# Pooling's softmax weights spread to channels in fp32, and the gram blocks handed from VectorE to ScalarE and GpSimd

## The chip, the cores and the metric

The kernel runs on one core of one Trainium2 chip. The metric is the device time of one execution in microseconds (us), the median of several runs. The trace is that of one profiled execution; all its times are counted from the start of its span.

## The reference

The input is 128 batches of 64 channels by 750 time points. A first layer (`tok`) pads time to 752, cuts it into 94 windows of 8, takes a score for each time point (64 channels times one weight vector, plus a bias), a softmax over the 8 points of a window, and sums the 8 points with those weights:

```python
scores = jnp.einsum('bwkf,of->bwko', xp, w) + b
weights = jax.nn.softmax(scores, axis=2)
pooled = jnp.sum(xp * weights, axis=2)          # 128 x 94 x 64
```

The pooled tokens go through a layer norm, q, k and v projections, an attention of 8 heads that mixes plain, squared and Grassmann scores (which need an orthogonalisation of q and k, and so their gram matrices), a second layer norm and a routed feed-forward network. All of it is fp32. The change touches the pooling and the gram matrices only.

## The kernel before

The program is a row of blocks with a barrier of all engines between them: `constants`, `pool_project`, `orthogonalise`, `attend`. The change is in `pool_project`, with its selector prepared in `constants`.

Two batches of 64 channels make a pair of 128 partitions; there are 64 pairs, in 4 groups of 16. A group's input (`x_g`, two buffers) comes by four DMAs of four pairs each on SyncE's queue. TensorE forms the scores of a group (`score_pair`, line 50), ScalarE copies them out with the bias, VectorE and ScalarE make the softmax of the group at once in `soft`, 64 rows of 376 time points: row 32·half + batch holds one half of the time of one of the group's 32 batches.

The loop of `pool_project` has 32 steps (and 4 more to empty it), two pairs to a step, an even and an odd one. In step i:

- TensorE's `spread` (line 386) carries the weights of one pair from the rows of `soft` to the 64 channels of each of its batches, by a product with a selector of zeros and ones, `pair_sel`: 128 channels, two halves of 376 columns, each in a bank of its own of `ps_spread`. It is called for the even pair, then for the odd one. In the first three groups, while n is below 10, it is followed by one or two score pairs of the next group.
- VectorE multiplies the even pair by the spread weights in PSUM (`product`, line 589) and sums the windows of 8 (`pooled`, line 593). ScalarE copies the odd pair's weights out (`w_odd`, line 493), GpSimd multiplies (line 557), VectorE sums these a step later.
- Each two steps a chunk c of 4 pairs passes the layer norm and the projection, in stages: `centre` (line 398, TensorE) at odd steps; squares and a copy (`j_xc`) on ScalarE; `variance` (404), the square root `j_std` on ScalarE (507), its inverse on VectorE (606), `rows` (415) twice and VectorE's scaled copy into `tok` (618) twice at the even step after; `grams` (427) at the next odd step, 8 gram blocks of 8 by 8 per pair column in `ps_c`.
- The gram blocks stand inside larger products. VectorE's `gram_own` (625) multiplies 256 columns of `ps_c` by `mask4`, and `gram_sum` (630) adds the four groups into `gram`. The next chunk's `centre` overwrites `ps_c`, so it waits for `gram_own`.
- SyncE stores each chunk's `tok` to DRAM by three DMAs, and at the end of the block waits for the last.

Each engine runs its instructions in the order written; the order within a step is TensorE: spread (even), variance and rows 0 or grams, spread (odd), rows 1 or centre; VectorE: product, inverse and rows, pooled odd, gram_own, pads, pooled even, gram_sum, rows, and at i % 8 in (4, 5) the two parts of the next group's softmax.

The weights are fp32 and the products of `spread` are bf16. So `parted` splits them exactly into three bf16 parts: ScalarE writes "hi" (line 456), GpSimd the remainder (459), ScalarE "mid" (462) and its copy to rows 64 to 127 (464), GpSimd "lo" (467). `spread` then makes, for each half, two accumulating products of 128 rows with a 128-row selector. For the first group this chain stands ahead of the first `spread`; for the others it runs at steps i % 8 of 5 and 6.

Of the kernel before, what the change touches and what calls it, by code (L numbers as in the profile page):

```python
# [22 lines left out]
WIN = 8  # L23
# [31 lines left out]
def constants(nc, p, x_g, x_in, ps_score, k):  # L55

    sem = nc.semaphore
    with ExitStack() as ctx:
# [11 lines left out]
        row_sel = ctx.enter_context(nc.sbuf_tensor("row_sel", [128, 2, 32], F32))  # L70
# [36 lines left out]
        def _(pool):  # L107
# [180 lines left out]
def pool_project(nc, x, x_g, x_in, ps_score, tokens, gram, v_dram, qk_dram, top_dram, qk_rows, rows_in, k):  # L288
# [4 lines left out]
    with ExitStack() as ctx:  # L293
        names = ("lo_zero scores_done scores_out maxima shifted exps sums_done inv_done weights_done hi_done rest_done "
                 "mid_done mid_moved lo_done spread_done even_done even_pooled odd_out odd_done odd_pooled "
                 "ready cent_done squared kept var_done std_done rstd_done tok_done gram_done gram_owned")
# [3 lines left out]
        biased = [drained[h] if EVICT[h] == "dve" else ctx.enter_context(sem(f"biased{h}")) for h in range(2)]  # L300
# [7 lines left out]
        soft = sb("soft", [64, N // 2, WIN])  # L308
        rest = sb("rest", [64, HALF])
        mid = sb("mid", [64, HALF], BF16)  # L310
        stat = sb("stat", [64, 3, N // 2])
        parts = sb("parts", [128, 2, 2, HALF], BF16)
# [6 lines left out]
        own = sb("own", [128, 2 * CP, D, 4])  # L319
# [4 lines left out]
        flat = soft[:].rearrange("p w k -> p (w k)")  # L324
# [13 lines left out]
        def _(sp):  # L338
# [6 lines left out]
            def store(c):  # L345
                a, batches = c % 2, slice(2 * CP * c, 2 * CP * (c + 1))
                for h in range(2):
                    sp.wait_ge(biased[h], c + 1)
# [22 lines left out]
        def _(pe):  # L371
# [47 lines left out]
            def grams(c):  # L419
                for h in range(2):  # L420
                    pe.wait_ge(biased[h], c + 1)
# [9 lines left out]
            pe.wait_ge(s["lo_zero"], 1)  # L431
# [19 lines left out]
        def parted(eng, g, part):  # L451

            a = g % 2
            if part == "hi":
                eng.wait_ge(s["weights_done"], g + 1)
                eng.activation(parts[0:64, a, 0, :], flat, ACT.Copy).then_inc(s["hi_done"], 1)
            if part == "rest":
                eng.wait_ge(s["hi_done"], g + 1)
                eng.tensor_tensor(rest[:], flat, parts[0:64, a, 0, :], ALU.subtract).then_inc(s["rest_done"], 1)
            if part == "mid":  # L460
                eng.wait_ge(s["rest_done"], g + 1)
                eng.activation(mid[:], rest[:], ACT.Copy).then_inc(s["mid_done"], 1)
                eng.wait_ge(s["mid_done"], g + 1)
                eng.activation(parts[64:128, a, 0, :], mid[:], ACT.Copy).then_inc(s["mid_moved"], 1)
            if part == "lo":
                eng.wait_ge(s["mid_done"], g + 1)
                eng.tensor_tensor(parts[0:64, a, 1, :], rest[:], mid[:], ALU.subtract).then_inc(s["lo_done"], 1)  # L467

        @block.scalar
        def _(act):  # L470
            def softmax(g, part):
                if part == 0:
                    if g:
                        act.wait_ge(s["scores_done"], g)
                    for quarter in range(4):
                        rows = slice(32 * quarter, 32 * quarter + 32)
                        half, at = divmod(quarter, 2)
                        out = act.activation(flat[32 * half:32 * half + 32, at * (TP // 4):(at + 1) * (TP // 4)], ps_score[rows, 0:TP // 4],
                                             ACT.Identity, bias=k["tok_bias"][rows])
                    out.then_inc(s["scores_out"], 1)  # L480
                if part == 1:
                    act.wait_ge(s["shifted"], g + 1)
                    act.activation(soft[:], soft[:], ACT.Exp).then_inc(s["exps"], 1)
# [25 lines left out]
            def scaled(c, h):  # L509
                a = c % 2  # L510
                if h == 0:
                    act.wait_ge(s["rstd_done"], c + 1)
                if c >= 2:
                    act.wait_ge(stored[a], 48 * (c // 2))
                    act.wait_ge(s["gram_done"], c - 1)
                act.wait_ge(s["tok_done"], 2 * c + h + 1)
                for e in range(2):
                    for b in range(2):
                        r = 2 * h + e
                        out = act.activation(tok[:, a, r, b, :], ps_tok[:, b, 192 * e:192 * e + 192], ACT.Copy,  # L520
                                             scale=rstd[:, a, 2 * r + b:2 * r + b + 1])
                out.then_inc(drained[h], 1)

            for part in range(4):
                softmax(0, part)
            for i in range(STEPS + 4):
                c = chunk_at(i, 4)
                if c is not None:
                    deviation(c)
                    if EVICT[0] == "act":  # L530
                        scaled(c, 0)
                if i < STEPS:
                    odd_weights(i)
                if c is not None and EVICT[1] == "act":
                    scaled(c, 1)
# [3 lines left out]
                if i < STEPS - HP:  # L539
                    for part in {4: (0, 1), 5: (2,), 6: (3,)}.get(i % HP, ()):  # L540
# [3 lines left out]
        def _(pool):  # L544
            def bias(c, h):
                rows = tok[:, c % 2, 2 * h:2 * h + 2].rearrange("p r b f -> p (r b) f")
                pool.wait_ge(drained[h], c + 1)
                pool.tensor_tensor(rows, rows, k["bias_row"][:, 0:1, :].broadcast_to([NP, 4, 192]), ALU.add).then_inc(biased[h], 1)

            pool.memset(parts[64:128, :, 1, :], 0.0).then_inc(s["lo_zero"], 1)  # L550
            parted(pool, 0, "rest")
            parted(pool, 0, "lo")
            for i in range(STEPS + 4):
# [4 lines left out]
                c = chunk_at(i, 4)  # L558
                for h in range(2):
                    if c is not None and EVICT[h] == "act":  # L560
                        bias(c, h)
# [1005 lines left out]
```

## Time and profile before

| | |
|---|---|
| runs, us | 887.52, 888.25, 890.45 (median 888.25) |
| profiled execution, us | 884.84 |
| its span, us | 883.0 |
| mean granted clock of TensorE | 0.937 |
| busy, us (share of span) | TensorE 765.8 (87%), VectorE 721.0 (82%), GpSimd 492.6 (56%), ScalarE 447.0 (51%) |
| `pool_project` in the trace | about 26 to 230.5 us |

The profiled execution took 884.84 us, 1.84 us of it outside the span from the first to the last instruction, and lies 3.41 us under the median of the runs. Busy shares are means over blocks with different limits, so the block that the change touches is read by itself. A granted clock of 1.00 is TensorE's upper level (2.4 GHz), 0.50 its lower (1.2 GHz).

### The profile page before, as it was taken

The numbers are of one execution on the slowest core, as the hardware profiler recorded it, in microseconds if no ns is written. First come the engines' busy times: TensorE is split into PE (matmuls) and PEld (weight loads), VectorE is DVE, ScalarE is ACT, GpSimd is POOL, SyncE is SP. The second block draws the span as 40 slices with busy tenths as digits, with TensorE's granted clock in tenths as the row PEclk, the third lists the DMA queues.
The fourth block names the chain that finished last, engine by engine and source line by source line (L and its number), as shares of the span: only waits on it lengthen the run. The fifth ranks groups of instructions, "written<-read, shape, count | busy, mean of one in ns | idle before, by whom it ended". The sixth has DMA issues, their size and how long they took to land.

```text
span 883.0 us, 39788 instructions
## 1 busy us (share of the span) xinstructions
PE 765.8 (87%) x16837; PEld 565.1 (64%) x16837; DVE 721.0 (82%) x1408; ACT 447.0 (51%) x927; POOL 492.6 (56%) x532
## 2 busy tenths in 40 slices
PE   4488887666694599999999999999999999899994
PEld 2245444434674478877777778877777887466663
DVE  4388888885579589999999999999999999667772
ACT  2253424321344165565655565665565556477773
POOL 3233333331000578888888888888888887222220
PEclk9789899896697599999999999999999999899998
DMA  8756662662570122222222222222222221001111
GB/s 295 284 168 198 197 197 58 130 128 58 155 143 2 48 76 64 65 64 64 64 66 65 79 65 64 64 64 64 66 73 71 64 64 45 1 22 29 28 29 33
DMA packets 89197, 77.63 MB, mean 88 GB/s; under 512 B 37145, under 2 KB 79708, under 8 KB 89052
## 3 DMA queue, kind: packets, MB, share of 16 engines
q1 hardware_dynamic: 88524, 73.83, 28.9%
q8 instruction: 131, 2.15, 1.0%
q10 hardware_dynamic: 528, 1.54, 0.5%
q14 instruction: 14, 0.11, 0.0%
HBM read 59.23 MB, written 13.04 MB: 82 GB/s over the span
## 4 chain that ended last, share of the span: by engine, by line
PE 51%; DVE 10%; issue 3%; ACT 1%; POOL 0%; POOLq 0%; ACTq 0%; DVEq 0%
PE ps_dot L1116 10%; PE ps_m L1140 8%; PE ps_a L1166 7%; PE ps_a L1158 7%; PE ps_a L1252 4%; DVE row_max_o L1376 3%; DVE row_max_e L1378 3%; PE ps_a L1129 3%; DVE row_max L1364 2%; PE ps_m L1102 2%; PE ps_a L1237 2%; DVE sums L1396 2%; PE ps_dot L1209 1%; PE ps_a L1260 1%; PE ps_dot L1227 1%
## 5 line engine op out<-in xcount | busy, mean ns | idle before, releaser
L1295 ACT ACTIVATE sq<-ps_dot 128x376 f32<-128x376 f32 x384 | 165.0, 482 | 158.4 <-PE ps_dot L1116 150.4
L1116 PE MATMUL ps_dot<-q_st,k_blk 64*64 64x94 f32 x6144 | 170.5, 249 | 1.1 <-ACT sq L1295 0.8
L1116 PEld LDWEIGHTS ps_dot<-q_st,k_blk 64*64 64x64 f32 x6144 | 134.6, 134 | 52.8 <-issue 28.8
L557 POOL TENSOR_TENSOR x_g<-x_g,w_odd 128x752 f32<-128x752 f32 x32 | 57.0, 1780 | 104.4 <-ACT w_odd L493 104.4
L1038 POOL TENSOR_TENSOR v_blk<-v_rep,vmask 128x384 f32<-128x384 f32 x128 | 106.6, 854 | 7.6 <-PE ps_m L1146 5.5
L1053 POOL TENSOR_TENSOR half<-prob 128x564 f32<-128x564 f32 x64 | 75.6, 1181 | 60.7 <-ACT prob L1290 60.7
L1060 POOL TENSOR_TENSOR k_blk<-k_cm,hmask 128x768 f32<-128x768 f32 x64 | 96.7, 1511 | 1.0 <-PE ps_a L1158 1.0
L1062 POOL TENSOR_TENSOR k_mix<-k_cm,cols 128x768 f32<-128x768 f32 x64 | 96.8, 1512 | 0.0
L1364 DVE TENSOR_REDUCE row_max<-ps_a 128x94 f32<-128x564 f32 x128 | 89.4, 740 | 4.5 <-PE ps_a L1166 4.4
L1166 PE MATMUL ps_a<-sq,mix_w 64*32 64x282 f32 x2048 | 81.8, 404 | 0.5 <-ACT sq L1295 0.5
L1140 PE MATMUL ps_m<-prob,v_blk 128*64 128x94 f32 x1536 | 76.6, 248 | 1.1 <-ACT prob L1290 1.1
L1287 ACT ACTIVATE prob<-prob,head_const 128x564 f32<-128x564 f32 x64 | 49.1, 767 | 51.7 <-DVE prob L1386 51.7
L1158 PE MATMUL ps_a<-q_st,k_mix 64*64 64x94 f32 x3072 | 74.3, 241 | 0.8 <-issue 0.4
L1140 PEld LDWEIGHTS ps_m<-prob,v_blk 128*64 128x64 f32 x1536 | 64.8, 136 | 8.7 <-ACT prob L1290 1.7
L1089 POOL COPY w_sel<-ffn_w 128x258 f32 x64 | 25.7, 402 | 79.5 <-DVE qk_rows L1452 54.2
L1158 PEld LDWEIGHTS ps_a<-q_st,k_mix 64*64 64x64 f32 x3072 | 67.2, 133 | 1.2 <-issue 1.1
L1371 DVE TENSOR_TENSOR k_blk<-ps_m,hmask 128x768 f32<-128x768 f32 x64 | 61.3, 957 | 7.5 <-PE ps_dot L1116 4.9
L386 PE MATMUL ps_spread<-parts,pair_sel 128*128 128x376 bf16 x256 | 58.4, 356 | 10.0 <-POOL parts L467 10.0
L493 ACT ACTIVATE w_odd<-ps_spread 128x752 f32<-128x752 f32 x32 | 25.5, 797 | 80.8 <-PE ps_spread L386 80.6
L1046 POOL TENSOR_TENSOR m_blk<-m_t,mask 128x128 f32<-128x128 f32 x64 | 25.8, 404 | 63.9 <-POOLq L706 63.9
L1396 DVE TENSOR_REDUCE sums<-half 128x94 f32<-128x282 f32 x128 | 59.8, 469 | 1.7 <-POOL half L1053 1.7
L593 DVE TENSOR_REDUCE tokens<-x_g 128x94 f32<-128x752 f32 x64 | 59.0, 925 | 0.6 <-POOL x_g L557 0.4
(219 smaller groups left out, 1450.7 us busy)
## 6 DMA issues: line engine op xcount, KB each, us to landing
v_rep<-v_rows SPq DMA_DIRECT2D x128, 192.0 KB, 3.1
x_g<-in_x_dram SPq DMA_DIRECT2D x15, 1500.0 KB, 6.5
qk_rows_kept<-tok SPq DMA_DIRECT2D x16, 384.0 KB
qk_rows<-qk_rows_kept SPq DMA_DIRECT2D x4, 1536.0 KB, 11.2
v_rows<-tok SPq DMA_DIRECT2D x16, 192.0 KB
q_st<-q_cm SPq DMA_DIRECT2D x64, 47.0 KB, 1.8
out_dram<-rows SPq DMA_DIRECT2D x16, 188.0 KB
x_g<-in_x_dram ACTq DMA_DIRECT2D x1, 1500.0 KB, 7.1
```

The lines of the kernel that those rows point to most:

```text
L1038: vb = pool.tensor_tensor(v_blk[:, a, b].rearrange("p t (o d) -> p (t o) d", o=H), v_rep[:, a, b].rearrange("p (t o d) -> p (t o) d", o=H, ...
L1053: pool.tensor_tensor(half[:], prob[:, a, :, 0:3, :], prob[:, a, :, 3:6, :], ALU.add).then_inc(s["half_done"], 1)
L1060: pool.tensor_tensor(k_blk[:, a, :, 0], k_cm[:, span(i, 1), :].rearrange("p i (u m) -> p (i u) m", m=4).unsqueeze(2).broadcast_to([128, NT ...
L1062: pool.tensor_tensor(k_mix[:, a].rearrange("p t x o -> p (t x) o"), k_cm[:, span(i, 1), :].rearrange("p i m -> p (i m)").unsqueeze(2).broa ...
L1116: mm = pe.matmul(ps_dot[64 * v:64 * v + 64, (2 * g + b) % 3, N * c:N * c + N], k_blk[rows, a, SLOTS * (3 * v + g) + c].rearrange("p k h m ...
L1140: pe.matmul(ps_m[64 * b:64 * b + 64, AV_AT:AV_AT + N], v_blk[:, a, b, t, :], prob[:, a, b, t, :], start=(t == 0), stop=(t == NT - 1), skip ...
L1158: mm = pe.matmul(ps_a[half_of, BANK[b][t // 3], N * (t % 3):N * (t % 3) + N], k_mix[64 * b:64 * b + 64, a, t, 8 * w:8 * w + 8].rearrange(" ...
L1166: mm = pe.matmul(ps_a[32 * c:32 * c + 32, BANK[b][v], 0:3 * N], k["mix_w"][64 * v:64 * v + 64, :], sq[64 * v:64 * v + 64, b, c].rearrange( ...
L1295: act.activation(sq[:, b, :, g, :], ps_dot[:, (2 * g + b) % 3, 0:SLOTS * N].rearrange("p (c n) -> p c n", c=SLOTS), ACT.Square).then_inc(s ...
L1364: dve.tensor_reduce(top[:, b, :], bass.AP(ps_a[:].tensor, 1024 * b, [[4 * 512, 128], [1, N], [512, 2], [N, 3]]), AX.XY, ALU.max).then_inc( ...
L1371: dve.tensor_tensor(k_blk[:, a, :, 1], ps_m[:, KT_AT:KT_AT + NP].rearrange("p (u m) -> p u m", m=4).unsqueeze(2).broadcast_to([128, NT * S ...
L1396: dve.tensor_reduce(sums[:, b], half[:, b].rearrange("p t n -> p n t"), AX.X, ALU.add).then_inc(s["sums_done"], 1)
```

## The change

`pair_sel` becomes fp32, 64 rows of 16 by 128. `spread` makes one fp32 product per half, whose operands are the 32 rows of that half: half 0 on rows 0 to 31, half 1 on rows 32 to 63, each into its own bank as before. The splitting (`parted`, its five instructions a group, and a memset) goes away; `soft` gets a second buffer, since `spread` now reads it directly. ScalarE copies the 256 gram columns out of PSUM (`grams_out`, first in its odd step), GpSimd masks them in place and adds them in two halvings (`gram_sum`, after its product with the odd pair); `centre` waits for ScalarE's copy in place of VectorE's masked one. The choice of engine for the scaled copy (`EVICT`), which was VectorE for both halves, is written out as such.

```diff
@@ constants
-            for quarter in range(4):
-                diagonal(row_sel[32 * quarter:32 * quarter + 32, quarter % 2, :], 0, [[-1, 32]], 1)
+            for half in range(2):
+                diagonal(row_sel[32 * half:32 * half + 32, :], 0, [[-1, 32]], 1)
...
-            for half in range(2):
-                act.activation(k["pair_sel"][:, half].rearrange("p n (b c) -> p (n b) c", b=2),
-                               row_sel[:, half, :].unsqueeze(2).broadcast_to([128, 32, C]), ACT.Copy)
+            act.activation(k["pair_sel"][:].rearrange("p n (b c) -> p (n b) c", b=2),
+                           row_sel[:].unsqueeze(2).broadcast_to([64, 32, C]), ACT.Copy)
@@ pool_project, TensorE
-                    pe.wait_ge(s["mid_moved"], g + 1)
-                    pe.wait_ge(s["lo_done"], g + 1)
+                    pe.wait_ge(s["weights_done"], g + 1)
...
                 for half in range(2):
-                    for part in range(2):
-                        mm = pe.matmul(ps_spread[:, 2 * (n % 2) + half, 0:HALF], k["pair_sel"][:, half, n, :], parts[:, g % 2, part, :],
-                                       start=(part == 0), stop=(part == 1))
+                    mine = slice(32 * half, 32 * half + 32)
+                    mm = pe.matmul(ps_spread[:, 2 * (n % 2) + half, 0:HALF], k["pair_sel"][mine, n, :], flat[mine, g % 2, :], start=True, stop=True)
...
-                    pe.wait_ge(s["gram_owned"], c)
+                    pe.wait_ge(s["gram_out"], c)
@@ ScalarE
-                if part == 2:
-                    parted(act, g, "hi")
-                if part == 3:
-                    parted(act, g, "mid")
...
+            def grams_out(c):
+                act.wait_ge(s["gram_done"], c + 1)
+                if c:
+                    act.wait_ge(s["gram_summed"], c)
+                act.activation(own[:].rearrange("p b g e -> p (b g e)"), ps_c[:, 0:256], ACT.Copy).then_inc(s["gram_out"], 1)
...
             for i in range(STEPS + 4):
+                c = chunk_at(i, 5)
+                if c is not None:
+                    grams_out(c)
@@ GpSimd
-            parted(pool, 0, "rest")
-            parted(pool, 0, "lo")
+            def gram_sum(c):
+                pool.wait_ge(s["gram_out"], c + 1)
+                pool.tensor_tensor(own[:], own[:], k["mask4"][:].unsqueeze(1).unsqueeze(3).broadcast_to([128, 2 * CP, 4, D]), ALU.mult).then_inc(s["gram_owned"], 1)
+                pool.wait_ge(s["gram_owned"], c + 1)
+                pool.tensor_tensor(own[:, :, 0:2], own[:, :, 0:2], own[:, :, 2:4], ALU.add).then_inc(s["gram_halved"], 1)
+                pool.wait_ge(s["gram_halved"], c + 1)
+                pool.tensor_tensor(gram[:, span(c, 2 * CP), :], own[:, :, 0, :], own[:, :, 1, :], ALU.add).then_inc(s["gram_summed"], 1)
...
-                if i < STEPS - HP and i % HP == 5:
-                    parted(pool, i // HP + 1, "rest")
-                if i < STEPS - HP and i % HP == 6:
-                    parted(pool, i // HP + 1, "lo")
+                c = chunk_at(i, 5)
+                if c is not None:
+                    gram_sum(c)
@@ VectorE
-                c = chunk_at(i, 5)
-                if c is not None:
-                    gram_own(c)
...
-                c = chunk_at(i, 5)
-                if c is not None:
-                    gram_sum(c)
```

## Rows read from the trace of the kernel before

**Rows 1.** Busy time of each engine in three stretches of pooling (instructions, granted clock).
```profile
35.90:41.90 6.00, 6.00 (x63) 2.24 (x60) 3.28 (x4) 1.22 (x2) 1.78 (x1) 0.77 0.27 106
104.00:113.00 9.00, 7.82 (x32) 4.70 (x34) 6.86 (x15) 4.21 (x8) 2.87 (x3) 0.50 0.40 124
163.00:205.00 42.00, 29.58 (x425) 17.54 (x424) 35.01 (x72) 10.57 (x20) 14.23 (x8) 0.95 0.66 133
```

**Rows 2.** VectorE's waits, 35 to 205 us: total, times, longest.
```profile
DVE x_g L589 <- PE ps_spread L386: 14.5, 15, 4.7
```

**Rows 3.** Timeline at pooling's start: start us, us, what, idle before.
```profile
31.32 0.54 DVE L584 TENSOR_TENSOR soft<-soft,stat 64x376 f32<-64x376 f32 x1
...
34.01 0.89 POOL L467 TENSOR_TENSOR parts<-rest,mid 64x376 bf16<-64x376 f32 x1 [0.63 <-ACT mid L462]
...
35.14 1.41 PE L386 MATMUL ps_spread<-parts,pair_sel 128*128 128x376 bf16 x4 [10.00 <-POOL parts L467]
```

**Rows 4.** Timeline of one chunk without scores, steps 29 and 30.
```profile
192.00 0.92 DVE L589 TENSOR_TENSOR x_g<-x_g,ps_spread 128x752 f32<-128x752 f32 x1
...
192.18 0.75 PE L427 MATMUL ps_c<-tok 94*32 94x32 f32 x64 [1.58 <-issue]
...
192.87 0.81 PE L386 MATMUL ps_spread<-parts,pair_sel 128*128 128x376 bf16 x4
...
194.25 0.88 PE L398 MATMUL ps_c<-tokens,cent_w 128*128 128x384 f32 x2 [0.57 <-DVE own L625]
...
194.97 0.80 PE L386 MATMUL ps_spread<-parts,pair_sel 128*128 128x376 bf16 x4
...
195.80 0.94 DVE L589 TENSOR_TENSOR x_g<-x_g,ps_spread 128x752 f32<-128x752 f32 x1 [0.54 <-PE ps_spread L386]
...
196.86 0.89 PE L415 MATMUL ps_tok<-w_tok,j_xc 64*96 64x192 f32 x8
...
197.69 0.81 PE L386 MATMUL ps_spread<-parts,pair_sel 128*128 128x376 bf16 x4
197.90 1.39 DVE L618 SCALAR_TENSOR_TENSOR tok<-ps_tok,j_rstd,bias_row 96x192 f32<-96x192 f32 x4 [0.44 <-PE ps_tok L415]
...
202.39 0.92 DVE L589 TENSOR_TENSOR x_g<-x_g,ps_spread 128x752 f32<-128x752 f32 x1
```

**Rows 5.** Groups of instructions, forms apart, 20 to 240 us: busy, mean ns, idle before.
```profile
L501 ACT ACTIVATE j_xc<-ps_c 128x384 f32<-128x384 f32 x16 | 7.8, 486 | 0.0
L625 DVE TENSOR_TENSOR own<-ps_c,mask 128x256 f32<-128x256 f32 x16 | 6.6, 411 | 2.5 <-PE ps_c L427 2.5
```

**Rows 6.** Page, costliest groups: GpSimd's products in the attention.
```profile
L1038 POOL TENSOR_TENSOR v_blk<-v_rep,vmask 128x384 f32<-128x384 f32 x128 | 106.6, 854 | 7.6 <-PE ps_m L1146 5.5
L1046 POOL TENSOR_TENSOR m_blk<-m_t,mask 128x128 f32<-128x128 f32 x64 | 25.8, 404 | 63.9 <-POOLq L706 63.9
```

**Rows 7.** Timelines of two chunks with a softmax, steps 13, 14 and 22.
```profile
103.40 0.80 ACT L493 ACTIVATE w_odd<-ps_spread 128x752 f32<-128x752 f32 x1
...
104.96 1.62 PE L398 MATMUL ps_c<-tokens,cent_w 128*128 128x384 f32 x2 [1.60 <-DVE own L625]
...
107.87 0.94 DVE L589 TENSOR_TENSOR x_g<-x_g,ps_spread 128x752 f32<-128x752 f32 x1 [0.38 <-PE ps_spread L386]
...
110.66 1.39 DVE L618 SCALAR_TENSOR_TENSOR tok<-ps_tok,j_rstd,bias_row 96x192 f32<-96x192 f32 x4 [0.81 <-PE ps_tok L415]
...
155.27 0.20 DVE L606 RECIPROCAL j_rstd<-j_std 96x8 f32<-96x8 f32 x1 [1.31 <-ACT j_std L507]
```

**Rows 8.** TensorE's timeline in step 9, a step with scores.
```profile
81.59 0.84 PE L50 MATMUL ps_score<-x_g,score_w 128*32 128x188 f32 x16
82.37 0.91 PE L398 MATMUL ps_c<-tokens,cent_w 128*128 128x384 f32 x2
```

**Rows 9.** Timeline of the block's end and the barrier behind it.
```profile
227.34 0.42 DVE L630 TENSOR_REDUCE gram<-own 128x64 f32<-128x256 f32 x1
...
230.66 4.16 PE L871 MATMUL ps_turn<-ident,gram 128*128 128x128 f32 x16 [3.83 <-PEq L293]
```

More of the change, by code:

```diff
@@ L299, in pool_project @@
         drained = [ctx.enter_context(sem(f"drained{h}")) for h in range(2)]
-        biased = [drained[h] if EVICT[h] == "dve" else ctx.enter_context(sem(f"biased{h}")) for h in range(2)]
         def sb(name, shape, dt=F32):
@@ L318, in pool_project @@
         tok = sb("tok", [NP, 2, CP, 2, 192])
-        own = sb("own", [128, 2 * CP, D, 4])
+        own = sb("own", [128, 2 * CP, 4, D])
         ps_spread = ctx.enter_context(nc.psum_tensor("ps_spread", [128, 4, 512], F32))
@@ L449, in _ @@
                     centre(c)
[L451 to L467, printed above, removed]
         @block.scalar
@@ L474, in softmax @@
                         act.wait_ge(s["scores_done"], g)
+                    if g >= 2:
+                        act.wait_ge(s["spread_done"], GP * (g - 1))
                     for quarter in range(4):
@@ L477, in softmax @@
                         half, at = divmod(quarter, 2)
-                        out = act.activation(flat[32 * half:32 * half + 32, at * (TP // 4):(at + 1) * (TP // 4)], ps_score[rows, 0:TP // 4],
+                        out = act.activation(flat[32 * half:32 * half + 32, g % 2, at * (TP // 4):(at + 1) * (TP // 4)], ps_score[rows, 0:TP // 4],
                                              ACT.Identity, bias=k["tok_bias"][rows])
@@ L507, in deviation @@
                 act.activation(std[:], ps_c[0:NP, W:W + 2 * CP], ACT.Sqrt, bias=k["ln_eps"][0:NP, 0:1]).then_inc(s["std_done"], 1)
[L509 to L524, printed above, removed]
+            def grams_out(c):
[3 more added lines that the diff above has]
+                act.activation(own[:].rearrange("p b g e -> p (b g e)"), ps_c[:, 0:256], ACT.Copy).then_inc(s["gram_out"], 1)
+            for part in range(2):
                 softmax(0, part)
             for i in range(STEPS + 4):
+                c = chunk_at(i, 5)
+                if c is not None:
+                    grams_out(c)
                 c = chunk_at(i, 4)
@@ L539, in _ @@
                 if i < STEPS - HP:
-                    for part in {4: (0, 1), 5: (2,), 6: (3,)}.get(i % HP, ()):
+                    for part in range(2 if i % HP == 4 else 0):
                         softmax(i // HP + 1, part)
@@ L557, in _ @@
                     pool.tensor_tensor(odd, odd, w_odd[:, i % 2, :], ALU.mult).then_inc(s["odd_done"], 1)
[L558 to L561, printed above, removed]
-                if i < STEPS - HP and i % HP == 5:
-                    parted(pool, i // HP + 1, "rest")
-                if i < STEPS - HP and i % HP == 6:
-                    parted(pool, i // HP + 1, "lo")
+                c = chunk_at(i, 5)
+                if c is not None:
+                    gram_sum(c)
         @block.vector
@@ L574, in softmax @@
                     dve.wait_ge(s["scores_out"], g + 1)
-                    dve.tensor_reduce(stat[:, 0, :], soft[:], AX.X, ALU.max).then_inc(s["maxima"], 1)
+                    dve.tensor_reduce(stat[:, 0, :], soft[:, g % 2], AX.X, ALU.max).then_inc(s["maxima"], 1)
                     dve.wait_ge(s["maxima"], g + 1)
-                    dve.tensor_tensor(soft[:], soft[:], over(stat[:, 0, :]), ALU.subtract).then_inc(s["shifted"], 1)
+                    dve.tensor_tensor(soft[:, g % 2], soft[:, g % 2], over(stat[:, 0, :]), ALU.subtract).then_inc(s["shifted"], 1)
                 if part == 1:
                     dve.wait_ge(s["exps"], g + 1)
-                    dve.tensor_reduce(stat[:, 1, :], soft[:], AX.X, ALU.add).then_inc(s["sums_done"], 1)
+                    dve.tensor_reduce(stat[:, 1, :], soft[:, g % 2], AX.X, ALU.add).then_inc(s["sums_done"], 1)
                     dve.wait_ge(s["sums_done"], g + 1)
@@ L583, in softmax @@
                     dve.wait_ge(s["inv_done"], g + 1)
-                    dve.tensor_tensor(soft[:], soft[:], over(stat[:, 2, :]), ALU.mult).then_inc(s["weights_done"], 1)
+                    dve.tensor_tensor(soft[:, g % 2], soft[:, g % 2], over(stat[:, 2, :]), ALU.mult).then_inc(s["weights_done"], 1)
             def product(i):
@@ L621, in rows_out @@
                 out.then_inc(drained[h], 1)
-            def gram_own(c):
-                dve.wait_ge(s["gram_done"], c + 1)
-                dve.tensor_tensor(own[:], ps_c[:, 0:256].rearrange("p (b g e) -> p b e g", g=4, e=D),
-                                  k["mask4"][:].unsqueeze(1).unsqueeze(1).broadcast_to([128, 2 * CP, D, 4]), ALU.mult).then_inc(s["gram_owned"], 1)
-            def gram_sum(c):
-                dve.wait_ge(s["gram_owned"], c + 1)
-                dve.tensor_reduce(gram[:, span(c, 2 * CP), :], own[:], AX.X, ALU.add)
             softmax(0, 0)
@@ L639, in _ @@
                     inverse(c)
-                    if EVICT[0] == "dve":
-                        rows_out(c, 0)
+                    rows_out(c, 0)
                 if 1 <= i <= STEPS:
                     pooled(i - 1, 1)
-                c = chunk_at(i, 5)
-                if c is not None:
-                    gram_own(c)
                 c = chunk_at(i, 2)
@@ L651, in _ @@
                     pooled(i, 0)
-                c = chunk_at(i, 5)
+                c = chunk_at(i, 4)
                 if c is not None:
-                    gram_sum(c)
-                c = chunk_at(i, 4)
-                if c is not None and EVICT[1] == "dve":
                     rows_out(c, 1)
@@ L659, in _ @@
                     softmax(i // HP + 1, i % HP - 4)
-EVICT = ("dve", "dve")
 def span(c, n):
@@ L1498, in audio_layer @@
             k["score_w"] = first.enter_context(nc.sbuf_tensor("score_w", [128, GP, 32], F32))
-            k["pair_sel"] = first.enter_context(nc.sbuf_tensor("pair_sel", [128, 2, GP, 128], BF16))
+            k["pair_sel"] = first.enter_context(nc.sbuf_tensor("pair_sel", [64, GP, 128], F32))
             ps_score = first.enter_context(nc.psum_tensor("ps_score", [128, 512], F32))
```

30 lines of the change are left out of this document (8 added, 22 removed).

## The prediction

> **What bounds the kernel now.** The chain that ended last reaches back only to 297 us and doesn't enter pooling, so I read pooling by windows first, then by VectorE's waits, then by the order of time in single chunks. From 163 to 205 us VectorE is busy 35.01 of 42.00 us, TensorE 29.58, GpSimd 14.23, ScalarE 10.57 [rows 1]. The reader is to see an engine that is nearly full and yet waits: VectorE lost 14.5 us in 15 waits before `product`, all for `spread` [rows 2]. The rows of one chunk say why [rows 4]. From the product of step 29 (192.00) to that of step 31 (202.39) is a period of 10.39 us. `centre` starts at 194.25, 0.57 us after TensorE was free, when VectorE's `gram_own` is over; the next `spread` stands behind it (194.97), and the next product, at 195.80, has waited 0.54. What follows from `centre` (squares, variance, rows) ends in `rows_out` at 197.90, after 0.44 more. So the period is a ring: VectorE's copies let `grams` start, then spread, gram_own, centre, rows, and VectorE again. Only what shortens this ring shortens the period, not every microsecond taken from VectorE.
>
> Two stretches differ. Before the first chunk TensorE is busy 6.00 of 6.00 us [rows 1]: there it is the bound. And at the start TensorE waits 10.00 us, the last part of it for the splitting: the weights are ready at 31.32 + 0.54 = 31.86, `lo` ends at 34.90, `spread` starts at 35.14 [rows 3].
>
> **The start.** Without the splitting `spread` can follow the weights at about 31.9: 3.2 us earlier. It runs at the lower clock there (1.41 us against 0.81) and will be 0.1 longer, see below. **-3.1 us.** Next due is the second group's input, for the scores behind each spread: from 35.9 us on TensorE is busy without a gap [rows 1], so it was there by then; that it is there 3 us sooner no row shows, and if it weren't the term would be 0.
>
> **The new spread.** Before: four bf16 records of 376 columns, 0.81 us start to end [rows 4]. The trace has no fp32 product of 32 rows. Nearest rows: `centre`, fp32, leaves two records of 384 columns per product, 0.88 us start to end and 0.72 to the next start, or 0.94 ns a column. Two fp32 products of 376 columns one after the other would be 4 x 0.35, about 1.55 us start to end; side by side 0.87. Which of the two, the `rows` product tells: eight fp32 records of 192 columns, in two tiles of 64 rows with a bank each, took 0.89 us [rows 4], where 8 x 0.18 = 1.44 would be their time in turn. They run in pairs. I take 0.87, 0.06 longer than before, and keep 1.55 for the rival.
>
> The shape of the tile changes too. `rows` to `spread` is 0.83 us (196.86 to 197.69) for 4 x 192 columns, which at centre's pace take 0.72: 0.11 us go into a change from 64-row tiles to 128 [rows 4]. Before, `centre`, both spreads around it and `variance` had 128 rows and columns for one another; now each passage is such a change, three more in a chunk, two of them ahead of `variance`.
>
> The Trainium skill (TensorEngine Tiling (Array Packing), Key Properties) says that changing the tiling mode drains the engine, while changing the tile within a mode doesn't. The 0.11 us agrees in kind; if a whole drain were the 0.16 us by which `centre` ends after the next record has started (0.88 - 0.72), two a chunk would cost 0.1 us more than by the row, 1.6 us over 16 chunks, and the sum below would be -5.2.
>
> **Early, TensorE bound.** Some nine spreads by 0.06 and two changes around the first `centre` by 0.11: **+0.8 us**. Bounds 0 and 1.6.
>
> **Chunks without scores.** After the change `centre` waits for ScalarE's copy. `grams` ends at 192.93; the copy of 256 columns costs at most the 0.49 of 384 columns [rows 5], so it is over by 193.45 and hidden by `spread`. `centre` then starts behind it: 192.87 + 0.71 + 0.11 = 193.69 in place of 194.25, 0.56 earlier. Squares, variance and rows follow `centre` with the same delays, so `rows_out` and the period lose 0.56. VectorE has 0.41 + 0.41 less to do; 0.26 of this becomes waiting. Three chunks are of this kind (steps 25, 27, 29): -1.7. In two (7, 15) the even step has scores ahead of `variance`, so the longer spread and its change (0.17) are on the ring: -0.39 each. **-2.5 us.**
>
> **Chunks with scores.** In step 9 `centre` (82.37) follows the score without a wait [rows 8]: gram_own is no part of the ring. What remains are two longer spreads and one more change: +0.23, in steps 9 and 17. In 11 and 19 half as many scores stand there, some of the wait for gram_own is left, and I take +0.1. **+0.7 us**, bounds -0.3 and +1.4.
>
> **Chunks with a softmax (steps 5, 13, 21).** Here `centre` waits 1.60 us for gram_own, as it has the softmax behind it on VectorE [rows 7]. After: ScalarE's copy takes the place that `w_odd` has now, 103.40, right after the exponential; with 0.49 `centre` can start at 103.95 in place of 104.96. `w_odd` moves back 0.4 to 0.5, and GpSimd behind it; the sum that needs them comes a step later. In steps 5 and 13 TensorE has the lower clock (0.50 from 104 to 113 [rows 1], `centre` 1.62 against 0.88), so the added 0.17 doubles: -1.01 + 0.34, and a little more as the copy is shorter than 0.49: -0.75 each. In step 21 the clock is up; there VectorE waits 1.31 for the square root [rows 7], which stands behind `hi` in ScalarE's queue. `hi` goes and `centre` is earlier, so this wait and the two gram instructions (0.74 to 0.82) go: -1.9. **-3.4 us**, bounds -1.5 and -7 (the last if steps 5 and 13 behave as 21).
>
> **Chunks at the lower clock without softmax (23, 31).** `centre` has no wait for gram_own there; spreads and changes at double price: **+0.7 us**.
>
> **At nothing.** GpSimd: three instructions of 256, 128 and 64 columns, by 0.85 (384 columns) and 0.40 (128) [rows 6] between 1.2 and 1.7 us a chunk; in 163 to 205 us it is idle 27.8 of 42, four chunks add 6.6. They stand between two products with the odd pairs; the cover is the wait for `w_odd`, and were it gone, 0.6 us a chunk would delay the odd sums. The splitting at later groups: ready some 3 us before it is needed. The selector in `constants`: ScalarE then waits for the scores anyway. The end: gram_sum on VectorE ends at 227.76, the next block starts at 230.66, held by SyncE's wait for the last store; ScalarE and GpSimd would end near 229 [rows 9]. If the barrier waited for them instead, +1.5.
>
> **The sum.** -3.1 + 0.8 - 2.5 + 0.7 - 3.4 + 0.7 = -6.8 us. Against the profiled execution: 884.84 - 6.8 = 878.0. The median of the runs lies 3.41 us higher, so I expect a median of 888.25 - 6.8 = **881.4 us**. With all added TensorE prices at nothing it would be -10, with twice these prices -3.6: the forecast's own range is 878 to 885.
>
> **Rivals.**
>
> *The halves run in turn* (slower). For it: no row has 32-row tiles, nor only two products in a row; against it: the pairs in `rows`. A spread then costs 0.66 to 0.7 us more. On the ring or on the full TensorE: ten early spreads (6.6), two in each of four chunks with scores (5.3), two at double price in steps 5 and 13 (5.3), five chunks without scores that go from -0.56 to about +0.5 (5.3), steps 21, 23 and 31 (4.5): +27, in all +20, about 908 us. If the second record of the first half overlaps the first of the second (three slots for four), half of it: +6.7, 895 us. It decides from 0.17 us a spread on (6.8 / 27 x 0.66).
>
> *TensorE becomes the bound* (no change). VectorE is relieved, but another part of the ring, such as `variance` behind the longer spread, takes all that the chunks give, -5.9. Left are -3.1 + 0.8 + 0.7 + 0.7 = -0.9: 887 us. For it speaks that in chunks with scores TensorE already has no gap ahead of `centre` [rows 8]; against it the 0.57 and 1.60 us of idle TensorE in the others [rows 4, 7].
>
> *The clock stays up.* Steps 5 and 13 have the lower clock after TensorE sat idle 1.60 us ahead of `centre` and longer before `grams`. With the idle time shorter the clock may not fall: two chunks then give 1.9 and not 0.75, step 23 gains 1 to 2: -4 more, 877 us. Against it: the other gaps of those steps stay, and 32-row tiles may equally leave it low for longer, at about 1.2 us a stretch.
>
> **How the numbers follow.** Forecast 0.60, clock stays up 0.12, TensorE the bound 0.14, halves in turn 0.14 (half of it partly). A change of 0.3%, 2.7 us, is about what a measurement of this kernel can tell from none. Faster by more: the forecast less its upper end, and the third rival, 0.68. Within: the second rival and that upper end, 0.18. Slower: 0.14. The range 875 to 891 holds the forecast, both middle rivals and the bounds, and leaves out most of the halves in turn.
>
> **What would show it.** First `spread` at about 32 us. A spread of 0.85 to 0.95 us at the upper clock with the second half's record starting within some 10 ns of the first's; over 1.2 proves the first rival. No-score periods of 9.8 us; `centre` there right behind `spread`, not behind ScalarE. GpSimd's gram work of 1.2 to 1.7 us inside its wait for `w_odd`. Next block 6 to 8 us earlier than 230.66. The prediction is wrong if periods don't shrink while `centre` starts earlier: then the ring is another one.

## The result and the profile after

| | before | after |
|---|---|---|
| median of the runs, us | 888.87 (4 runs, 887.52 to 890.45) | 928.28 (4 runs, 920.98 to 935.78) |
| profiled execution, us | 884.84 | 921.21 |
| its span, us | 883.0 | 919.3 |
| mean granted clock of TensorE | 0.937 | 0.874 |
| first `spread`, us | 35.14 | 33.15 |
| next block starts, us | 230.66 | 266.80 |

The change made the kernel slower: ratio 1.0362, interval 1.0330 to 1.0393. The prediction (881.4, range 875 to 891) was wrong in sign. Two of the four runs after, those at 935 us with a clock of 0.855 and 0.862, are left out of the ratio. The span grew by 36.3 us and the start of the next block moved by 36.1, so nearly all of it was lost ahead of that start, although the first `spread` came 2.0 us earlier.

The page of after, its row of TensorE's granted clock (40 slices of 23 us), and then windows of after, those of [rows 1] and two more; each line gives the window, its length, the busy time of TensorE, its weight loads, VectorE, ScalarE and GpSimd, the granted clock, and the DMA's share and GB/s:

```profile
PEclk9555958655559859999999999999999999999998
```

```profile
35.90:41.90 6.00, 6.00 (x36) 1.89 (x34) 2.59 (x4) 0.80 (x1) 1.77 (x1) 0.50 0.23 92
104.00:113.00 9.00, 8.21 (x140) 4.71 (x142) 6.75 (x13) 2.47 (x6) 4.83 (x5) 1.00 0.78 242
163.00:205.00 42.00, 40.24 (x352) 21.20 (x352) 28.40 (x55) 14.31 (x26) 16.07 (x18) 0.58 0.39 84
...
35.90:60.00 24.10, 24.10 (x145) 8.78 (x144) 9.79 (x12) 5.34 (x7) 7.07 (x4) 0.50 0.25 87
...
180.00:220.00 40.00, 39.66 (x318) 19.96 (x316) 24.44 (x49) 8.98 (x18) 14.65 (x15) 0.50 0.58 121
```

From 163 to 205 us the clock was 0.95 before, with TensorE busy 29.58 us and VectorE 35.01 [rows 1]; now it is 0.58, TensorE is busy 40.24 and VectorE 28.40. The bound has passed to TensorE. From 36 to 60 us TensorE has no gap at all (24.10 of 24.10 us) and keeps its lower level, 1.2 GHz, throughout. The kernel before, in the same stretch:

```profile
35.90:60.00 24.10, 20.86 (x266) 10.15 (x264) 19.44 (x31) 10.64 (x16) 10.22 (x6) 0.92 0.46 158
```

The clock of after isn't low everywhere: from 104 to 113 us it is 1.00, where before was at 0.50 in another step [rows 1]. Over the whole of pooling the mean is 0.61 after (35.9 to 264 us) and 0.86 before (35.9 to 230).

Was it the new product that took TensorE's time? The groups of TensorE's instructions in pooling, of before and then of after (busy us, mean ns, idle before):

```profile
L386 PE MATMUL ps_spread<-parts,pair_sel 128*128 128x376 bf16 x256 | 58.4, 356 | 10.0 <-POOL parts L467 10.0
L415 PE MATMUL ps_tok<-w_tok,j_xc 64*96 64x192 f32 x256 | 33.5, 387 | 10.2 <-DVE tok L618 9.9
L50 PE MATMUL ps_score<-x_g,score_w 128*32 128x188 f32 x440 | 24.5, 333 | 2.3 <-DMA x_g<-in_x_dram 2.3
L398 PE MATMUL ps_c<-tokens,cent_w 128*128 128x384 f32 x32 | 17.5, 637 | 8.5 <-DVE own L625 8.3
L404 PE MATMUL ps_c<-mean_w,j_sq 128*96 128x2 f32 x128 | 15.1, 239 | 3.2 <-ACT j_xc L501 3.2
```

```profile
L378 PE MATMUL ps_spread<-soft,pair_sel 32*128 32x376 f32 x256 | 89.8, 792 | 6.8 <-DVE soft L539 6.8
L406 PE MATMUL ps_tok<-w_tok,j_xc 64*96 64x192 f32 x256 | 45.5, 498 | 4.1 <-DVE tok L573 3.8
L50 PE MATMUL ps_score<-x_g,score_w 128*32 128x188 f32 x440 | 33.4, 431 | 1.1 <-DMA x_g<-in_x_dram 1.1
L389 PE MATMUL ps_c<-tokens,cent_w 128*128 128x384 f32 x32 | 23.0, 816 | 1.0 <-ACT own L483 1.0
L395 PE MATMUL ps_c<-mean_w,j_sq 128*96 128x2 f32 x128 | 20.6, 283 | 1.9 <-ACT j_xc L471 1.9
```

The four groups that the change doesn't touch took 90.6 us and take 122.5: +31.9, beside +31.4 of `spread`. Instructions that stayed the same and grew by a third point to the clock. (Busy time grew by more than the 36 us lost, as part of it fills time in which TensorE was idle before.)

Now a chunk as in [rows 4], step 25 of after, where the clock is 0.50, and step 9 of after at the upper level, which answers to [rows 8] (timelines):

```profile
196.33 0.94 DVE L544 TENSOR_TENSOR x_g<-x_g,ps_spread 128x752 f32<-128x752 f32 x1
...
197.38 1.62 PE L378 MATMUL ps_spread<-soft,pair_sel 32*128 32x376 f32 x4
197.51 0.38 ACT L483 ACTIVATE own<-ps_c 128x256 f32<-128x256 f32 x1 [3.57 <-PE ps_c L418]
198.94 1.65 PE L389 MATMUL ps_c<-tokens,cent_w 128*128 128x384 f32 x2
...
202.19 0.94 DVE L544 TENSOR_TENSOR x_g<-x_g,ps_spread 128x752 f32<-128x752 f32 x1 [3.23 <-PE ps_spread L378]
...
209.83 0.94 DVE L544 TENSOR_TENSOR x_g<-x_g,ps_spread 128x752 f32<-128x752 f32 x1
```

```profile
98.36 0.91 PE L389 MATMUL ps_c<-tokens,cent_w 128*128 128x384 f32 x2
99.20 0.90 PE L378 MATMUL ps_spread<-soft,pair_sel 32*128 32x376 f32 x4
100.04 0.84 PE L50 MATMUL ps_score<-x_g,score_w 128*32 128x188 f32 x16
```

`grams`' copy is over 197.51 + 0.38 = 197.89, hidden by `spread`, and `centre` follows without a wait, as the prediction had it. At the upper level a spread takes 0.90 us; at the lower 1.62. The period, 196.33 to 209.83, is 13.50 us where it was 10.39 [rows 4], and VectorE waits 3.23 us for `spread` in place of 0.54.

VectorE's waits for `spread` from 35 to 205 us answer to [rows 2] (14.5 us in 15), the groups of the gram work to [rows 6] and the end to [rows 9]:

```profile
DVE x_g L544 <- PE ps_spread L378: 33.5, 13, 4.3
```

```profile
L507 POOL TENSOR_TENSOR own<-own,mask 128x256 f32<-128x256 f32 x15 | 9.7, 648 | 7.8 <-ACT own L483 7.8
L509 POOL TENSOR_TENSOR own<-own 128x128 f32<-128x128 f32 x15 | 7.0, 468 | 1.2
L511 POOL TENSOR_TENSOR gram<-own 128x64 f32<-128x64 f32 x15 | 4.8, 317 | 1.2
...
L483 ACT ACTIVATE own<-ps_c 128x256 f32<-128x256 f32 x15 | 5.7, 383 | 49.2 <-PE ps_c L418 49.1
```

```profile
264.70 0.32 POOL L511 TENSOR_TENSOR gram<-own 128x64 f32<-128x64 f32 x1
...
266.80 1.54 PE L807 MATMUL ps_turn<-ident,gram 128*128 128x128 f32 x5 [3.84 <-PEq L291]
```

### The profile page after: what moved, and what is told of

Read it like the earlier page. It is cut to its first block, busy times and chain, and to the rows that moved or that the text cites. A ratio compares the mean times of both kernels' runs of the same rounds, so it can differ in the third digit from the quotient of the medians.

```text
span 919.3 us, 39808 instructions
## 1 busy us (share of the span) xinstructions
PE 830.0 (90%) x16837; PEld 587.7 (64%) x16837; DVE 713.0 (78%) x1376; ACT 445.5 (48%) x930; POOL 506.4 (55%) x569
## 4 chain that ended last, share of the span: by engine, by line
PE 48%; DVE 10%; issue 3%; ACT 1%; POOL 0%; POOLq 0%; ACTq 0%; DVEq 0%
PE ps_dot L1052 9%; PE ps_m L1076 8%; PE ps_a L1102 7%; PE ps_a L1094 7%; PE ps_a L1188 3%; DVE row_max_o L1312 3%; DVE row_max_e L1314 3%; PE ps_a L1065 3%; DVE row_max L1300 2%; DVE sums L1332 2%; PE ps_m L1038 2%; PE ps_a L1173 1%; PE ps_dot L1145 1%; PE ps_a L1196 1%; PE ps_m L1082 1%
## 5 line engine op out<-in xcount | busy, mean ns | idle before, releaser
L378 PE MATMUL ps_spread<-soft,pair_sel 32*128 32x376 f32 x256 | 89.8, 792 | 6.8 <-DVE soft L539 6.8
L544 DVE TENSOR_TENSOR x_g<-x_g,ps_spread 128x752 f32<-128x752 f32 x32 | 29.9, 934 | 40.6 <-PE ps_spread L378 39.9
L573 DVE SCALAR_TENSOR_TENSOR tok<-ps_tok,j_rstd,bias_row 96x192 f32<-96x192 f32 x128 | 44.4, 406 | 21.7 <-PE ps_tok L406 21.7
```

## The experiments

Each ratio is taken against runs of the kernel before in the same comparison, whose medians were 888.47 us (e1 to e4), 888.00 (e5 to e7) and 887.41 (e8 to e10).

Theory A: the spread that leaves 64 of TensorE's 128 rows out keeps the granted clock at its lower level, and everything on TensorE pays. Theory B: it is the fp32 product itself, its passes, weight loads or changes of tile shape. Theory C: moving the grams changed order and idle time, and so the clock.

### All 128 rows in use (e1_rows128)

After, with the weights on rows 0 to 31 and 64 to 95, and each half a tile of 64 rows; the 32 spare rows of a tile meet zeros in the selector. Columns, data type, weight loads and the records per spread stay; the height of a tile changes from 32 to 64 rows.

```diff
-                    mine = slice(32 * half, 32 * half + 32)
+                    mine = slice(64 * half, 64 * half + 64)
```

> The changed kernel with each half's 32 weight rows placed at the head of a tile of 64 rows (rows 0 to 31 and 64 to 95), the 32 rows behind them zeros in the selector: the two fp32 products of a spread now take all 128 rows of TensorE in place of 64, same columns, same order, same waits. Theory A (the granted clock falls as the new spread leaves half of the rows out): the clock stays at the upper level for most of pooling as before the change, and the time is what was predicted, 876 to 886 us. Theory B (fp32 itself, its weight loads or the more frequent changes of tile shape bring the clock down): nothing changes, 915 to 935 us, with the lower clock in about three quarters of pooling.

892.91 us (9 runs, 888.29 to 895.99), ratio 1.0045, interval 1.0017 to 1.0073, clock 0.913. That is slower than the 876 to 886 that theory A forecast, but by the ratios (1.0362 and 1.0045) 28 of the 32 us are gone. Its stretch from 36 to 60 us and one chunk without scores at the upper level:

```profile
35.90:60.00 24.10, 21.78 (x260) 10.34 (x260) 19.54 (x33) 11.79 (x20) 10.84 (x7) 0.92 0.52 168
```

```profile
197.35 0.90 PE L378 MATMUL ps_spread<-soft,pair_sel 64*128 64x376 f32 x4
198.19 0.91 PE L389 MATMUL ps_c<-tokens,cent_w 128*128 128x384 f32 x2
199.03 0.90 PE L378 MATMUL ps_spread<-soft,pair_sel 64*128 64x376 f32 x4
```

A spread takes the same 0.90 us as with 32-row tiles, so no time was saved in the product itself: the clock is what differs, 0.92 against 0.50. What keeps this kernel from the forecast is the clock too. From 39 to 149.3 us it fell only for up to about 9 us at a time, as before's did; then it fell for 37.6 us, where before's fall of that place, from about 158 to 165 us, lasted some 7 (windows):

```profile
140.00:149.30 9.30, 6.97 (x133) 4.48 (x126) 7.90 (x17) 5.25 (x10) 3.57 (x5) 1.00 0.15 34
149.30:186.90 37.60, 35.36 (x259) 19.51 (x262) 25.40 (x51) 9.77 (x18) 14.88 (x15) 0.50 0.40 86
```

Ahead of the fall TensorE was busy 6.97 of 9.30 us; after it, 35.36 of 37.60. The no-score periods are 13.57 and 13.49 us in the low stretch, 9.89 and 9.87 behind it.

### The old bf16 product on half the rows (e2_before64)

Before, whose products take rows 0 to 63 alone; this leaves out the middle part of the weights.

```diff
-                        mm = pe.matmul(ps_spread[...], k["pair_sel"][:, half, n, :], parts[:, g % 2, part, :],
+                        mm = pe.matmul(ps_spread[...], k["pair_sel"][0:64, half, n, :], parts[0:64, g % 2, part, :],
```

> The kernel before, with its bf16 products of spread on rows 0 to 63 alone (the mid part of the weights is left out; hi and lo stay): as many products and columns, no fp32, no other edit. Theory A: the lower clock takes over in pooling here too and the time rises by 20 us or more, to 905 to 930. Theory B: unchanged within 3 us, 886 to 892.

916.8 us (4 runs, 906.45 to 921.48), ratio 1.0283, interval 1.0225 to 1.0341, clock 0.868:

```profile
35.90:60.00 24.10, 24.10 (x153) 8.30 (x151) 10.85 (x13) 5.34 (x7) 7.07 (x4) 0.50 0.26 92
```

No fp32 spread, no moved grams, no products side by side, the same number of products and columns: the clock falls as in after. This execution was the longest of the four; the others had 0.876 to 0.891, against 0.928 to 0.944 for before. A change of tile shape does come in with the 64-row product, but e1 has 64-row tiles between 128-row products too, with all rows in use, and 0.92 in this window. B and C are not needed for the loss.

### The spread alone and the grams alone (e3_spread_only, e4_grams_only)

After with the grams as before on VectorE; and before with the grams moved as in the diff.

```diff
-                    pe.wait_ge(s["gram_out"], c)
+                    pe.wait_ge(s["gram_owned"], c)
```

> The changed kernel with the grams masked and summed by VectorE as before: the fp32 spread alone. Theory A: the clock of the changed kernel, as the spread is the cause, 920 to 940 us, a few us over the changed kernel or equal to it. Theory C (moving the grams shifted the order of work and so the idle times on which the clock depends): the clock recovers, 880 to 895 us.

> The kernel before with the grams alone moved to ScalarE and GpSimd, bf16 spread and splitting kept. By the prediction's steps the ring of a chunk without scores is 0.6 us shorter (no shape change is added here), chunks with a softmax 1 to 2 us, chunks with scores 0 to 0.2: -6 to -9 us, 880 to 883. Theory C: the clock falls, 915 us or more. If VectorE's relief is all turned into waits: 887 to 890.

The spread alone: 937.54 us (4 runs, 928.57 to 955.32), ratio 1.0494, interval 1.0434 to 1.0554, clock 0.852. The grams alone: 884.08 us (12 runs, 878.34 to 887.58), ratio 0.9940, interval 0.9915 to 0.9964, clock 0.934. The two parts have opposite signs. C falls: the moved grams gain 4.4 us by the medians (5.3 by the ratio), somewhat less than the 6 to 9 expected, and their clock is before's.

### Do the zeros matter? (e5_signed)

As e1_rows128, with +1 and -1 in the selector's spare rows, which cancel.

```diff
+                step(pool.memset(spare, 1.0))
+                step(pool.affine_select(out=spare, in_=spare, compare_op=ALU.is_ge, fill=-1.0, base=-16,
+                                        pattern=[[0, 32]], channel_multiplier=1))
```

> The kernel with two tiles of 64 rows again, but the selector's 32 spare rows of each tile hold +1 (16 rows) and -1 (16 rows) in place of zeros; the spare rows of the weights are all equal, so their share adds up to nothing. Open is why 64-row tiles still have more of the lower clock than the kernel before (0.913 against 0.937) and 893 in place of 881 us. If it is the zeros, the clock comes up to 0.93 or more and the time to 876 to 886 us. If rows in use count whatever stands in them, it stays at 889 to 896, and the rest is to be looked for in the tile shapes or the order of work.

891.22 us (10 runs, 886.47 to 896.05), ratio 1.0044, interval 1.0020 to 1.0069, clock 0.917: as with zeros in the selector. (The spare rows of `soft` hold the softmax of zeros, 1/8 each, in both.) What the selector has in the spare rows makes no difference that these runs can tell; values of the weights in those rows were not varied.

### The splitting hidden at the start only (e6_grams_first)

e4_grams_only, in which the first four pairs are spread in fp32 from two 64-row tiles while the splitting runs beside them. For that `soft` has two buffers and its halves stand at rows 0 and 64, as in e1.

```diff
+                    if g == 0 and n < FIRST:
+                        mine = slice(64 * half, 64 * half + 64)
+                        mm = pe.matmul(ps_spread[...], k["first_sel"][mine, n, :], flat[mine, 0, :], start=True, stop=True)
+                        continue
```

> The kernel before with the grams moved, and in addition the first four pairs alone spread in fp32 from two tiles of 64 rows, so that they need not wait for the splitting, which runs beside them; from the fifth pair on the bf16 products with all rows. The start should come 2 to 3 us earlier than with the grams alone, the clock stay as in the kernel before: 879 to 883 us, ratio about 0.991. If the start is taken back by later waits: 884 as with the grams alone.

881.38 us (7 runs, 874.87 to 882.61), ratio 0.9905, interval 0.9871 to 0.9938, clock 0.939. Against e4 that is 0.0035 of 888 us, about 3.1 us, the size that the prediction gave to the start; the two intervals overlap, so these runs don't prove the gain.

### The halves in turn, on all rows (e7_in_turn)

After with the rows of e1_rows128, but each half an fp32 product over one tile of 128 x 128, with zeros in the selector for the other half's rows. The two halves then run one after the other: this is the first rival of the prediction, built as a kernel.

```diff
-                    mm = pe.matmul(ps_spread[...], k["pair_sel"][mine, n, :], flat[mine, g % 2, :], start=True, stop=True)
+                    mm = pe.matmul(ps_spread[...], k["pair_sel"][:, half, n, :], flat[:, g % 2, :], start=True, stop=True)
```

> The changed kernel with each half's fp32 product over all 128 rows in one tile of 128 by 128 (zeros in the selector outside the half's 32 rows): the two halves must run in turn, and there is no change of tile shape around the centre and variance products. Theory A (rows left out bring the clock down): the clock stays up, a spread takes about 1.55 us, and the time is that of the prediction's rival for halves in turn, 900 to 912 us. If fp32 products bring the clock down by themselves: more than 930 us, a spread of 2.9 us at the lower level.

887.63 us (10 runs, 885.48 to 889.54), ratio 0.9994, interval 0.9973 to 1.0014, clock 0.953; the 900 to 912 that was expected was too much. Two of its windows, and a spread ahead of `centre`:

```profile
35.90:60.00 24.10, 24.10 (x192) 12.34 (x185) 14.12 (x22) 7.68 (x13) 8.36 (x5) 0.95 0.27 92
...
38.20:212.00 173.80, 162.80 (x1904) 95.02 (x1902) 131.03 (x251) 62.30 (x113) 76.27 (x73) 1.00 0.51 141
```

```profile
175.66 1.53 PE L378 MATMUL ps_spread<-soft,pair_sel 128*128 128x376 f32 x4
177.02 0.81 PE L389 MATMUL ps_c<-tokens,cent_w 128*128 128x384 f32 x2
```

The same stretch, TensorE busy the same 24.10 of 24.10 us, fp32 products of 376 columns in both kernels: 0.50 after, 0.95 here. A spread of 1.53 us in place of 0.90 makes a kernel that is some 33 us faster (ratios 0.9994 and 1.0362), since from 38 to 212 us the clock is 1.00 without a break. B falls: e7 has the fp32 products and their passes, e1 the changes of tile shape besides, and neither has the clock of after.

### TensorE's idle time filled (e8_rows128_fill, e9_after_fill, e10_best_fill)

One fp32 product of 128 rows into `ps_c`, whose result nobody reads, stands ahead of `grams` (324 columns, 160 in steps with scores) and, in steps without scores, ahead of the second `rows` (160). In e8 this is added to e1_rows128, in e9 to after, in e10 to e6_grams_first.

```diff
+            def fill(c, columns):
+                pe.wait_ge(s["std_done"], c + 1)
+                pe.matmul(ps_c[:, 0:columns], k["ident"][:], k["w_bd"][:].rearrange("p s f -> p (s f)")[:, 0:columns],
+                          start=True, stop=True)
...
+                        fill(c, 160)
...
+                fill(c, 160 if i < STEPS - HP and i % HP < 5 else 324)
```

> The kernel with two tiles of 64 rows, and idle TensorE filled: one extra fp32 product of 128 rows whose result nobody reads (324 columns ahead of grams, 160 where scores stand in the step, and 160 ahead of the second rows product in steps without scores), put where TensorE waits for VectorE's copies anyway. If that idle time is what still lets the clock fall with all rows in use, the clock stays up through pooling, no-score periods are 9.9 us throughout and the time is 876 to 882 us. If it isn't, 889 to 896 us, with the stretches of the lower clock after steps 5, 13 and 21 as before.

> The changed kernel (tiles of 32 rows) with the same filling products and nothing else. If rows left out by the spread bring the clock down (theory A), the filling, a tenth of TensorE's time, repairs little: 910 to 935 us, clock below 0.89. If idle time had been the cause, the clock recovers and the time is that of the prediction, 876 to 886 us.

> The kernel before with the grams moved and the first four pairs in fp32, with the same filling products. Its six stretches of the lower clock in pooling cost about 1 us each; if they go, 875 to 879 us and a clock of 0.95 or more; if not, 880 to 883 us as without the filling.

| kernel | us (runs) | ratio, interval | clock |
|---|---|---|---|
| e8_rows128_fill | 875.47 (4: 872.67 to 876.32) | 0.9854, 0.9818 to 0.9891 | 0.949 |
| e9_after_fill | 927.34 (4: 911.76 to 928.0) | none given | 0.874 |
| e10_best_fill | 874.58 (6: 867.97 to 877.16) | 0.9849, 0.9811 to 0.9886 | 0.958 |

A window of e1_rows128 and the same one of e8_rows128_fill, then three of e9_after_fill:

```profile
36.90:197.00 160.10, 139.30 (x1751) 76.68 (x1750) 121.00 (x232) 57.71 (x102) 68.44 (x65) 0.82 0.52 145
...
36.90:197.00 160.10, 137.33 (x1940) 76.90 (x1940) 131.38 (x250) 62.74 (x113) 74.97 (x72) 1.00 0.56 154
```

```profile
35.90:60.00 24.10, 24.10 (x148) 8.36 (x140) 10.60 (x13) 5.34 (x7) 7.08 (x4) 0.50 0.28 100
100.00:140.00 40.00, 36.36 (x536) 19.57 (x534) 32.18 (x63) 16.26 (x30) 17.87 (x19) 1.00 0.67 212
180.00:220.00 40.00, 40.00 (x303) 20.42 (x294) 19.58 (x39) 8.54 (x17) 12.89 (x14) 0.50 0.58 120
```

With all rows in use the filling lifts e1_rows128 from 0.82 to 1.00 over the same 160 us and gains 17 us (ratios 1.0045 and 0.9854). With 32-row tiles the runs, 911.76 to 928.0 us against 920.98 to 935.78 for after, show no gain beyond their scatter: the upper level holds from 100 to 140 us, but in the other two windows TensorE has no idle time that could be filled (24.10 of 24.10 us, 40.00 of 40.00) and is at 0.50 all the same. e10_best_fill beats both kernels, by 13 us against before in the same comparison (887.41 - 874.58); e8 does so by 12. Against e6, without the filling, e10's gain is about 5 us by the ratios, and their intervals overlap a little.

## Why the prediction was wrong

**The step that failed** is "The new spread". It weighed how long the product lasts at a given clock (+0.06 us a spread) and let the clock be that of before, stretch by stretch; in its place the mean clock of pooling fell from 0.86 to 0.61, and what the change doesn't touch on TensorE got longer with it (90.6 us to 122.5). That rows left out bear on the clock came up only against the third rival: "32-row tiles may equally leave it low for longer, at about 1.2 us a stretch". The kind was right there and the size wrong: the low stretches did not grow by some us, they became most of pooling. e1 (rows back, same times, 0.92 in place of 0.50 from 36 to 60 us) and e2 (rows taken from the old product, 0.50) show the cause from both sides. Over all the kernels, from 36 to 60 us, the four whose spread takes 64 rows (after, e2, e3, e9) have 0.50, and the eight others 0.87 to 1.00.

**The ring was right at the upper level, in the chunks whose clock before was up too.** Periods between VectorE's `product` in odd steps, each the difference of two starts in the timelines, us; those of e8 and of e1 where its clock was up:

```
chunk of step      5      7      9      11     13     21     25-29
before             12.40  10.45  10.93  11.80  12.44  11.65  10.39
after (mixed)      11.63  15.42  11.22  11.92  12.62  12.61  13.5
e1, upper level      -    10.12  11.22  11.93    -      -    9.87-9.89
e8                 10.04  10.12  11.22  11.93  10.04  10.03  9.86-9.87
predicted change   -0.75  -0.39  +0.23  +0.10  -0.75  -1.9   -0.56
e8 less before     -2.36  -0.33  +0.29  +0.13  -2.40  -1.62  -0.53
```

In chunks 5 and 13 the prediction kept before's lower clock and named -7 for all three softmax chunks if they behaved as step 21, although three times its own -1.9 is -5.7; at the upper level they give -6.4. The filling of e8 stands in these periods too.

**The start** was sized right and partly lost ahead of it. Rows of after's timelines that answer to [rows 3]:

```profile
22.80 2.73 PE L50 MATMUL ps_score<-x_g,score_w 128*32 128x188 f32 x32 [1.14 <-DMA x_g<-in_x_dram]
...
32.51 0.54 DVE L539 TENSOR_TENSOR soft<-soft,stat 64x376 f32<-64x376 f32 x1
...
33.15 1.62 PE L378 MATMUL ps_spread<-soft,pair_sel 32*128 32x376 f32 x4 [6.82 <-DVE soft L539]
```

The first `spread` follows the weights by 0.10 us in place of 3.28 us (32.51 + 0.54 = 33.05, 33.15; before 31.86, 35.14), as forecast, but the weights are 1.19 us later than before's 31.86: the last score products of the block ahead took 2.73 us at the lower level, where before's took 1.48. Those products are the same in both kernels; why the clock fell there in this execution is open (e6's first spread is at 31.62).

**Side by side** held: 0.90 us, 0.87 predicted, and the two halves' first records start within 0.01 us of each other. The 0.11 us for a change of tile height held too: in e1, where `rows` and `spread` both have 64-row tiles, `spread` starts 0.73 us behind `rows` (200.83, 201.56), where it was 0.83 before. **GpSimd's gram work** is 0.648 + 0.468 + 0.317 = 1.43 us a chunk (1.2 to 1.7), ScalarE's copy 0.38, and the end doesn't wait for them: they are over at 264.70 + 0.32 = 265.02, and the next block starts at 266.80, 4.02 us after SyncE issued its last store (262.78), as before (226.64 and 230.66). e4 shows the moved part's worth: -4.4 us.

**The rivals.** "TensorE becomes the bound" came about, at the lower clock and not by the price that it was given. "The halves in turn" was priced at +20 over before; as a kernel (e7), it costs nothing that can be measured (887.63 against 888.00). Its price of a spread was near (0.63 us more, for 0.66 to 0.7), that of the chunks too high: against e8, +1.06 in each of those of steps 9 and 11 (12.28 and 12.99, for 1.32), +0.5 in those of 25 to 29 (10.36, for 1.06). What it left out is again the clock, which stays up in chunks 5 and 13 (9.94 each). So the rival that was feared is the better of the two forms, and the one that was hoped for the worse.

By the time of the product alone the packed form won: 0.90 us against 1.53. By the time of the kernel it lost: 1.0362 of before's against 0.9994. The Trainium skill (TensorEngine Tiling (Array Packing), Overview) offers independent tiles as the remedy for a contraction of 64 rows or fewer, which leaves the array poorly used. The trace agrees on the product and differs on the kernel, where 32-row tiles in two of four places left half the rows out; there the measurement decides.

**What stays open.** Why 64-row tiles in pairs (e1, 0.913) hold the clock less well than one tile of 128 rows in turn (e7, 0.953): e1 has more idle time, and filling it helps, but idle time and tile shape were not separated. Why the clock of the half-row kernels comes back at all: in after it is 1.00 from 95.5 to 116.5 and from 145.5 to 168.5 us, in e2 from 96.5 to 118 and from 144 to 171, in both about steps 9 to 12 and 17 to 20, where score products stand beside the work of a chunk. So half the rows don't hold the lower level everywhere, and what lifts it was not tested. Four 32-row tiles, two pairs of batches at once on all rows, were not tried.

## What to carry to other kernels

A product on part of the rows can cost more than a longer one that fills the other rows with zeros (e7 against after, some 33 us): price it by its time and by the granted clock of everything around it, and look at the clock row of the changed kernel before any chain of waits. Treat the clock of a stretch as something that a change can move, not as a property of the place. Where TensorE is not the bound, a few full-row products in its idle time can be worth more than the instructions that were saved elsewhere (e8 against e1, 17 us).

## What the runs showed of the hardware that was not expected

With TensorE busy 24.10 us of 24.10 (36 to 60 us) the granted clock was 0.50 where the spread took 64 of 128 rows, in fp32 (after) and in bf16 (e2), and 0.95 where it took all (e7). A full engine is no sign of its upper level: from 180 to 220 us after was busy 39.66 us at 0.50, e1_rows128 29.53 at 0.76. Zeros in the spare selector rows were as good as +1 and -1 (mean clock 0.913 and 0.917). And the clock makes runs of one kernel scatter: the two ends of e10's six runs, 867.97 and 877.16 us, had 0.964 and 0.947.
